# Cross attention in one core: the last key's term as one fp32r product for each half of the output

## What is computed

```python
xn = _layernorm(x, ln_gamma, ln_beta)
q = (xn @ w_q).reshape(B, SQ, NUM_HEADS, DIM_HEAD)
kv = context @ w_kv
k, v = jnp.split(kv, 2, axis=-1)
...
scores = jnp.einsum('bqhd,bkhd->bhqk', q * SCALE, k)
attn = jax.nn.softmax(scores, axis=-1)
out = jnp.einsum('bhqk,bkhd->bqhd', attn, v).reshape(B, SQ, INNER)
out = out @ w_out + b_out
```

## Time and profile before

| | us |
|---|---|
| median of three runs (lowest, highest) | 1835.36 (1833.28, 1838.26) |
| the profiled execution | 1835.1 |
| its span, first to last instruction | 1833.3 |
| TensorE busy | 1797.8 (98%) |
| VectorE busy | 1120.9 (61%) |
| ScalarE busy | 666.9 (36%) |
| GpSimd busy | 557.6 (30%) |

### The profile page before, as it was taken

One profiled execution on the slowest core, in us unless ns is written; L12 is line 12 of the kernel. 1 busy time (PEld: TensorE's weight loads), 2 busy tenths in 40 slices (PEclk: granted clock), 3 DMA queues, 4 the chain that ended last, 5 costly groups with the idle time before them and its releaser, 6 DMA issues.

```text
span 1833.3 us, 36324 instructions
## 1 busy us (share of the span) xinstructions
PE 1797.8 (98%) x13584; PEld 1547.6 (84%) x13584; DVE 1120.9 (61%) x2271; ACT 666.9 (36%) x1356; POOL 557.6 (30%) x546
## 2 busy tenths in 40 slices
PE   5999999999999999999999999999999999999999
PEld 4878988998899899889988997788887788888887
DVE  6636567666756765676667666788889733333322
ACT  2245444544454554445444544311112411111111
POOL 3024534544454355335434545411121000000000
PEclk9999999999999999999999999999999999999999
DMA  7325434543544354345434447432440502010100
GB/s 254 127 97 145 128 112 121 145 125 93 147 126 124 105 149 134 107 126 148 116 102 139 128 117 244 140 90 83 126 130 22 177 8 69 1 69 0 46 1 23
DMA packets 236118, 199.16 MB, mean 109 GB/s; under 512 B 12768, under 2 KB 193376, under 8 KB 236064
## 3 DMA queue, kind: packets, MB, share of 16 engines
q1 hardware_dynamic: 231632, 189.78, 35.8%
q10 hardware_dynamic: 4432, 8.65, 1.3%
HBM read 131.01 MB, written 33.82 MB: 90 GB/s over the span
## 4 chain that ended last, share of the span: by engine, by line
PE 90%; DVE 2%; DMA 1%; SPq 0%; issue 0%; POOL 0%; ACT 0%; DVEq 0%; POOLq 0%; ACTq 0%
PE s_ps L83 25%; PE s_ps L84 24%; PE s_ps L85 24%; PE s_ps L579 7%; PE s_ps L634 6%; PE s_ps L641 1%; PE s_ps L1365 1%; PE s_ps L1376 1%; PE s_ps L1307 0%; DMA a_m_xn<-x 0%; DMA a_xin<-x 0%; PE s_ps L588 0%; PE s_ps L1387 0%; PE s_ps L1356 0%; DMA o_lo<-x_o_lo 0%
## 5 line engine op out<-in xcount | busy, mean ns | idle before, releaser
L83 PE MATMUL s_ps<-w_cT_hi,w_space_hi 128*128 128x258 f32 x1024 | 293.3, 286 | 0.2 <-DVE w_space_lo L725 0.2
L84 PE MATMUL s_ps<-w_cT_lo,w_space_hi 128*128 128x258 f32 x1024 | 289.9, 283 | 0.0
L85 PE MATMUL s_ps<-w_cT_hi,w_space_lo 128*128 128x258 f32 x1024 | 288.3, 282 | 0.0
L530 POOL TENSOR_TENSOR x_prob<-x_prob,x_share 128x256 f32<-128x256 f32 x256 | 155.6, 613 | 338.4 <-DVE x_share L692 330.2
L718 DVE COPY x_mix<-s_ps 128x512 f32<-128x512 f32 x256 | 174.5, 687 | 68.6 <-PE s_ps L85 66.1
L83 PE MATMUL s_ps<-x_pT_hi,x_cn_hi 128*128 128x512 f32 x512 | 206.0, 402 | 4.0 <-DVE x_mix L718 4.0
L850 ACT ACTIVATE x_prob<-s_ps,x_negmax 128x257 f32<-128x257 f32 x256 | 121.9, 476 | 240.2 <-DVE x_negmax L687 237.0
L85 PE MATMUL s_ps<-x_pT_hi,x_cn_lo 128*128 128x512 f32 x512 | 201.4, 393 | 0.0
L84 PE MATMUL s_ps<-x_pT_lo,x_cn_hi 128*128 128x512 f32 x512 | 200.8, 392 | 0.0
L83 PEld LDWEIGHTS s_ps<-w_cT_hi,w_space_hi 128*128 128x128 f32 x1024 | 193.4, 189 | 6.2 <-issue 3.8
L84 PEld LDWEIGHTS s_ps<-w_cT_lo,w_space_hi 128*128 128x128 f32 x1024 | 193.9, 189 | 0.7
(11 more groups left out here) (204 smaller groups left out, 3526.7 us busy)
## 6 DMA issues: line engine op xcount, KB each, us to landing
e_raw_T<-ctx_T SPq DMA_DIRECT2D x64, 514.0 KB, 4.6
e_raw_n<-ctx_nat SPq DMA_DIRECT2D x64, 512.0 KB, 3.9
x_prob_T<-x_blocks SPq DMA_DIRECT2D x256, 128.0 KB, 2.7
q<-q_q ACTq DMA_DIRECT2D x16, 512.0 KB, 2.8
e_q<-q SPq DMA_DIRECT2D x16, 512.0 KB, 4.1
o_hi<-x_o_hi SPq DMA_DIRECT2D x32, 256.0 KB, 2.7
o_lo<-x_o_lo SPq DMA_DIRECT2D x32, 256.0 KB, 3.7
a_oT_hi<-o_hi SPq DMA_DIRECT2D x16, 512.0 KB, 4.2
```

What stands on the lines that cost most here:

```text
L83: pe.matmul(out, lhs[0], rhs[0], start=start, stop=False)
L84: pe.matmul(out, lhs[0], rhs[1], start=False, stop=False)
L85: return pe.matmul(out, lhs[1], rhs[0], start=False, stop=stop)
L530: pool.tensor_tensor(prob[:, i, 0:KT * P], prob[:, i, 0:KT * P], share[:, i:i + 1].to_broadcast([P, KT * P]), ALU.mult)\
```

## The change

The sixteen last-key products of a turn become two, one for each half. A product has 128 rows of contraction, of which 96 are used: `last_v` has, for each of four groups of heads and each of two (`l`), twelve rows: three for each of four batches. The three rows hold the high part of the values, the low part and the high part again, as `v_dram` now has them; the matching rows of `last_p` hold the probability's high part twice and its low part. The sum over rows is then high x high, high x low, low x high. Columns are the 512 of the bank, rows of the result the 128 of a head pair. The product opens the accumulation of the whole bank (`start=True`), and the value products add to it.

Around it: GpSimd writes each last probability three times. VectorE rounds the turned probabilities to fp32r (`last_h`), takes the rest, with sign and place from the new table `last_rows`, and spreads half by half: the first in `keep_last`, the second behind `low_out(t, 0)`. Ahead of the loop VectorE takes the low part of the values and three DMAs write them. `load_v` has eight DMAs and stands behind `load_n(t, 2)`. `out_half(0)` waits first for the loads, for the third copy of mix 3 and for `last_p`, and for the fourth copy where it needs that chunk.

```diff
-    last_p = s.sb("last_p", [P, TILES, GB, SQ])
-    last_v = s.sb("last_v", [P, inner])
-    last_z, last_t = s.sb("last_z", [P, TILES, SQ]), s.sb("last_t", [P, TILES, SQ])
-    own = s.sb("own", [P, GB])
+    last_p = s.sb("last_p", [P, 2, PAIRS // 2, GB, SQ], F32R)
+    last_v = s.sb("last_v", [P, 2, P], F32R)
+    last_z, last_t = s.sb("last_z", [P, TILES, SQ // 2]), s.sb("last_t", [P, 2, SQ])
+    last_h = s.sb("last_h", [P, 2, SQ], F32R)
+    OWN = GB * PAIRS // 2
+    own = s.sb("own", [P, OWN + 1])
...
             sp.wait_ge(o_ready.sem, o_ready.at(t, 0))
+            rows = v_rows[bass.ds(t * GB * PARTS, GB * PARTS), :].rearrange("r (m l g e) -> r m l g e", m=2, l=2, g=HT)
             for g in range(HT):
-                dst = last_v[g * SQ:g * SQ + GB, :].rearrange("b (i g e) -> b i g e", g=HT, e=HE)[:, :, g, :]
-                src = v_dram[bass.ds(t * GB, GB), :].rearrange("b (i g e) -> b i g e", g=HT, e=HE)[:, :, g, :]
-                sp.dma_start(dst, src).then_inc(v_loaded.sem, 16)
+                for l in range(2):
+                    at, h = g * SQ + l * SQ // 2, g % 2
+                    sp.dma_start(f32(last_v[at:at + GB * PARTS, :, h * HE:(h + 1) * HE]), rows[:, :, l, g, :])\
+                        .then_inc(v_loaded.sem, 16)

...
         def turn(t, more):
-            load_v(t)
             if more:
...
             load_n(t, 2)
+            load_v(t)
             if more:
...
-        for g in range(HT):
-            sp.dma_start(own[g * SQ:(g + 1) * SQ, :], identity[0:SQ, 0:GB]).then_inc(own_loaded, 16)
+        sp.dma_start(own[:, :], last_rows).then_inc(own_loaded, 16)
...
-        sp.wait_ge(v_stored, 16)
+        sp.wait_ge(v_stored, 48)
...
-            pool.tensor_tensor(last_z[:, :, b % GB], prob[:, :, SK - 1], share[:, :], ALU.mult)\
+            at = b % GB * PARTS
+            pool.tensor_tensor(last_z[:, :, at:at + PARTS], prob[:, :, SK - 1:SK].to_broadcast([P, TILES, PARTS]),
+                               share[:, :].rearrange("p (i k) -> p i k", k=1).to_broadcast([P, TILES, PARTS]), ALU.mult)\
...
         def out_half(t, m):
+            if m == 0:
+                pe.wait_ge(v_loaded.sem, v_loaded.at(t, 16 * 2 * HT))
+                pe.wait_ge(mix_kept.sem, mix_kept.at(t, GB * DC - 1))
+            pe.wait_ge(last_kept.sem, last_kept.at(t, m + 1))
+            pe.matmul(ps[:, O_BANK[m], :], last_v[:, m, :], last_p[:, m, :, :, :].rearrange("p j b q -> p (j b q)"),
+                      start=True, stop=False)
             for j in range(4 * m, 4 * m + 4):
...
                 for c in range(DC):
-                    if j == 0:
-                        pe.wait_ge(mix_kept.sem, mix_kept.at(t, (GB - 1) * DC + max(c + 1, DC - 1)))
+                    if j == 0 and c == DC - 1:
+                        pe.wait_ge(mix_kept.sem, mix_kept.at(t, GB * DC))
                     for h in range(2):
                         n = 2 * j + h
-                        pe.matmul(out[h], w_v[:, c, n * HE:(n + 1) * HE], mix[:, c, :, place(n)],
-                                  start=c == 0, stop=False)
-                if j == 0:
-                    pe.wait_ge(v_loaded.sem, v_loaded.at(t, 16 * HT))
-                    pe.wait_ge(last_kept.sem, last_kept.at(t, 1))
-                for h in range(2):
-                    n = 2 * j + h
-                    mm = pe.matmul(out[h], last_v[:, n * HE:(n + 1) * HE],
-                                   last_p[:, n // HT, :, :].rearrange("p b q -> p (b q)"), start=False, stop=True)
+                        mm = pe.matmul(out[h], w_v[:, c, n * HE:(n + 1) * HE], mix[:, c, :, place(n)],
+                                       start=False, stop=j == 4 * m + 3 and c == DC - 1)
             mm.then_inc(o_ready.sem, 1)
...
             dve.wait_ge(last_ready.sem, last_ready.at(t, GB))
-            dve.transpose(last_t[:, :, :], last_z[:, :, :]).then_inc(last_turned.sem, 1)
+            dve.transpose(last_t[:, :, :], last_z[:, :, :].rearrange("p (m l) r -> p m (l r)", m=2))\
+                .then_inc(last_turned.sem, 1)
             dve.wait_ge(last_turned.sem, last_turned.at(t, 1))
+            dve.tensor_copy(last_h[:, :, :], last_t[:, :, :]).then_inc(last_turned.sem, 1)
+            dve.wait_ge(last_turned.sem, last_turned.at(t, 2))
+            dve.scalar_tensor_tensor(last_t[:, :, :], last_t[:, :, :], own[:, OWN:OWN + 1], f32(last_h[:, :, :]), ALU.mult,
+                                     ALU.add).then_inc(last_turned.sem, 1)
+            dve.wait_ge(last_turned.sem, last_turned.at(t, 3))
             dve.wait_ge(o_ready.sem, o_ready.at(t, 0))
-            dve.tensor_tensor(last_p[:, :, :, :],
-                              last_t[:, :, :].rearrange("p i (b q) -> p i b q", b=1).to_broadcast([P, TILES, GB, SQ]),
-                              own[:, :].rearrange("p (i b q) -> p i b q", i=1, q=1).to_broadcast([P, TILES, GB, SQ]),
+            spread_last(t, 0)
+
+        def spread_last(t, m):
+            shape = [P, OWN, SQ]
+            dve.tensor_tensor(last_p[:, m, :, :, :].rearrange("p j b q -> p (j b) q"),
+                              last_t[:, m, :].rearrange("p (x q) -> p x q", x=1).to_broadcast(shape),
+                              own[:, 0:OWN].rearrange("p (x q) -> p x q", q=1).to_broadcast(shape),
                               ALU.mult).then_inc(last_kept.sem, 1)
...
             low_out(t, 0)
+            spread_last(t, 1)
             if more:
...
-        dve.wait_ge(own_loaded, 16 * HT)
+        dve.wait_ge(own_loaded, 16)
+        dve.wait_ge(v_rounded, 1)
+        dve.tensor_tensor(all_last[1], ps[0:B, M_BANK[0]:M_BANK[0] + 2, :], f32(all_last[0]), ALU.subtract)\
+            .then_inc(v_copied, 1)
...
-        act.activation(all_last, ps[0:B, M_BANK[0]:M_BANK[0] + 2, :], ACT.Copy).then_inc(v_copied, 1)
+        act.activation(all_last[0], ps[0:B, M_BANK[0]:M_BANK[0] + 2, :], ACT.Copy).then_inc(v_rounded, 1)
+        act.wait_ge(v_rounded, 1)
+        for k in (0, 2):
+            act.dma_start(v_dram[:, k, :].rearrange("b (h n) -> b h n", h=2), f32(all_last[0])).then_inc(v_stored, 16)
...
-        act.dma_start(v_dram.rearrange("b (h n) -> b h n", h=2), all_last).then_inc(v_stored, 16)
+        act.dma_start(v_dram[:, 1, :].rearrange("b (h n) -> b h n", h=2), f32(all_last[1])).then_inc(v_stored, 16)
...
+    last_rows = np.zeros((4, 2, 16, 17), np.float32)
+    for g, l, b, k in itertools.product(range(4), range(2), range(4), range(3)):
+        last_rows[g, l, 3 * b + k, 4 * (2 * l + g // 2) + b] = -1 if k == 2 else 1
+        last_rows[g, l, 3 * b + k, 16] = -1 if k == 2 else 0
```

More of the change, by code:

```diff
@@ L374, in cross_attention @@
     share_done, probs_ready = s.count("share_done", GB * TILES), s.count("probs_ready", GB * TILES)
-    last_ready, last_turned = s.count("last_ready", GB), s.count("last_turned", 1)
+    last_ready, last_turned = s.count("last_ready", GB), s.count("last_turned", 3)
     turned = s.count("turned", GB * TILES)
@@ L378, in cross_attention @@
     pT_hi, pT_lo = s.count("pT_hi", GB * KT), s.count("pT_lo", GB * KT)
-    last_kept = s.count("last_kept", 1)
+    last_kept = s.count("last_kept", 2)
     mixed, mix_kept = s.count("mixed", GB * DC), s.count("mix_kept", GB * DC)
@@ L383, in cross_attention @@
     o_stored = s.count("o_stored", 64, 32)
-    l_loaded, v_ready, v_copied, v_stored = s.sem("l_loaded"), s.sem("v_ready"), s.sem("v_copied"), s.sem("v_stored")
-    all_last, lT = mix[0:B, 0, 0:2, :], mix[:, 1, 0, 0:DC * B].rearrange("p (c b) -> p c b", c=DC)
+    l_loaded, v_ready, v_rounded = s.sem("l_loaded"), s.sem("v_ready"), s.sem("v_rounded")
+    v_copied, v_stored = s.sem("v_copied"), s.sem("v_stored")
+    all_last, lT = [mix[0:B, 0, 2 * k:2 * k + 2, :].bitcast(F32R) for k in range(2)], mix[:, 1, 0, 0:DC * B].rearrange("p (c b) -> p c b", c=DC)
     slots = [wk[:, j, :] for j in range(PAIRS)]
@@ L556, in gpsimd @@
         pool.memset(last_z[:, :, :], 0.0)
-        for ap in [last_v[:, :]] + [f32(a[:, :, SK:SKE]) for c in cT for a in c]:
+        for ap in [f32(last_v[:, :, :])] + [f32(a[:, :, SK:SKE]) for c in cT for a in c]:
             last = pool.memset(ap, 0.0)
@@ L752, in turn @@
             invert(t, 1, 3)
[L753 removed]
+            dve.wait_ge(v_stored, 48)
             keep_mix(t, 0, 0)
@@ L1757, in build @@
 def build(nc, x, ctx_nat, ctx_T, last_T, gamma, beta, wq, wkT, wv, w_out, b_out, gate, aq, ak, av, wg, wu, wd,
-          identity, same_token, out):
+          identity, same_token, last_rows, out):
     tokens, dim = x.shape
@@ L1813 @@
 def kernel(**inputs):
+    import itertools
     import numpy as np
```

13 lines of the change are left out of this document (7 added, 6 removed).

## The result

The changed kernel took **1852.9 us** (median of 4 runs, 1850.3 to 1856.3) against 1834.4 us (1833.3 to 1838.3) of the kernel before on the same chip: 1.0094 times as long, 95% interval 1.0082 to 1.0106. The forecast was 1819 us, faster. It came out on the other side. The profiled execution took 1854.4 us, its span is 1852.3 us, 19.0 more than before.

A forecast was written before the change was run, and what follows sets the result against it. TensorE, busy in all of a 62.9 us turn, was taken as the bound. 15 turns x (1.50 gained - 0.30 waited) = 18.0, less 1.4 in the last turn, is 16.6 us off: 1819 us, range 1811 to 1831.

The forecast's parts named there:

- The removed and the added products: TensorE's output halves: four last-key pairs out, one 0.23 us product in; with a covered stall, 1.50 us gained a turn.
- Rival 4: Opening product of each output half costs 0.43 us instead of 0.23; 31 lose 6 us: 1825 us, chance 0.07.
- The stall in the first block: First output half, VectorE's last copy of `mix` late by 0.21 to 0.25 us; new product ahead gains 0.20 a turn.
- What VectorE gets: `keep_last` gains two steps, 0.5 us together, and a second spread comes behind `low_out(0)`; both covered by VectorE's idle time.
- The moved and doubled loads: Eight value loads hold SP 6.6 us, exchange of batch 2 goes 1.5 us late; TensorE waits 0.3 us a turn.
- rival 3: Eight issues hold SP longer than the products save, deciding from 7.8 us; up to 1857 us, slower; chance 0.06.
- Rival 2: Context of batch 2 lands late, so TensorE waits 1.0 or 1.5 us: 1829 us (chance 0.10) or 1836 (0.08).
- rival 1: Eight loads on SP are covered, issuing in under about 6.2 us, so no TensorE wait: 1814 us, chance 0.19.
- The last turn: No fold pairs hide the loads: exchange 2.7 us late, 2.0 count, 0.9 given back, 0.3 charged between halves; 1.4 lost.
- Ahead of the loop and in the first turn: VectorE's subtraction of 64x1024 values, about 1.3 us, runs beside the first score tiles: 0 counted (bounds 0 and 1.3).

## Why the prediction was wrong

**The removed and the added products: right, a little too good.** 1.50 us a turn were counted, and the kernels without a wait give 62.87 - 61.57 = 1.30. From the last mix product to the first value product 0.33 us passed before (626.77 to 627.10) and 0.71 pass now (697.21 to 697.92), so the opening product costs 0.38 us in the first half where 0.23 was taken. In the second half the same count gives 0.24 (709.28 to 709.73, against 639.53 to 639.74), as forecast: the 0.33 us behind the product there are what a 512-column fp32r product ahead of fp32 products took in the kernel before too. Rival 4 named this mechanism at 0.43 for both halves and priced it at 6 us; it came in one half of two, 0.15 us a turn of the 0.20 that are missing. The stall in the first block of the earlier trace rows did go: the 64 products take 3.65 and 3.64 us in the two halves (697.92 to 701.57, 709.73 to 713.37).

**What VectorE gets: right in the loop, wrong in the last turn.** `keep_last` and the spread are in VectorE's timeline:

```profile
691.14 0.20 DVE L740 CAST x_last_h<-x_last_t 128x64 fp32r<-128x64 f32 x1
691.37 0.28 DVE L742 SCALAR_TENSOR_TENSOR x_last_t<-x_last_t,x_own,x_last_h 128x64 f32<-128x64 f32 x1
691.78 0.69 DVE L750 TENSOR_TENSOR x_last_p<-x_last_t,x_own 128x512 fp32r<-128x512 f32 x1
...
694.89 0.69 DVE L725 COPY x_mix<-s_ps 128x512 f32<-128x512 f32 x1 [0.61 <-PE s_ps L85]
...
1135.16 1.06 DVE L740 CAST x_last_h<-x_last_t 128x64 fp32r<-128x64 f32 x1
1136.26 1.26 DVE L742 SCALAR_TENSOR_TENSOR x_last_t<-x_last_t,x_own,x_last_h 128x64 f32<-128x64 f32 x1
1137.55 1.66 DVE L750 TENSOR_TENSOR x_last_p<-x_last_t,x_own 128x512 fp32r<-128x512 f32 x1
```

In the loop the two added steps take 0.64 us (691.14 to 691.78) where 0.5 were forecast, and VectorE still idles 0.61 us behind them, as it had 0.69. In the last turn the same three steps take 1.06, 1.26 and 1.66 us instead of 0.20, 0.28 and 0.69. The prediction priced them nowhere in that turn, though the kernel before has a hint: its one spread took 1.48 us there, at 1123.38. They stand ahead of the copy that ends the wait of 2.38 us, and that wait is theirs and not the loads'. From TensorE's restart behind the wait before it to its end 5.39 us pass (1134.47 to 1139.86), and 5.37 to 5.40 in each of the other ten runs that have the three steps, with loads in that turn or without. In the kernel before with the eight loads, which lacks the two added steps, it is 2.90 us and there is no wait. Where the granted clock is low in that stretch the products fill more of the 5.4 us, and the wait shrinks to between 0.8 and 1.2 us, in one run to nothing.

**The moved and doubled loads: the step that failed, and in it one term.** The chain was laid out right: SP, exchange, ScalarE's probabilities, VectorE's `split_probs(2)` and copies, TensorE at the third chunk of the mix of batch 2. Its slack was right too: 1.5 us late gives 0.3 us, and the split loads in the kernel before measured 1.5 and 0.33. Wrong was the price of one issue. "The nearest rows for their pace are the four themselves", 0.83 us apart; but those had 4 partitions and the new ones have 12, and these came 0.99 apart. Eight of them hold the queue 7.92 us instead of 6.6, the 1.3 us have no cover left, and the wait is 1.35 us and 0.1 for the restart on top. The prediction's own threshold was close: it set the point of decision at 7.8 us, 0.98 each. At the measured 7.92 its rule gives a wait of 1.6 us and a turn 0.1 us longer; it is 0.29 longer, since the products gave 1.30 and not 1.50. The case had been rival 3, at 0.06. The row against it, the median of 0.64, was of loads of another shape; the 0.63 to 1.12 of its spread should have been the bound, with the chance to match.

That context and exchange together decide is seen in ScalarE's 2.50 and 0.56 us: the context's landing ended the longer idle time, and the exchange landed 0.56 us behind its rounding. Rival 2 took its delay from a slow landing; it came from the late issue.

The Trainium skill ("DMA: Bandwidth & Descriptors", Anatomy of one DMA) puts the sequencer's dispatch at about 50 ns, in a table on DMAs that GpSimd issues. The prediction took it over to loads that SyncE issues. The runs have 0.562 to 0.785 us for these, so it was no support for rival 1.

**The last turn: 1.4 us lost was forecast, some 9 measured.** The lateness of the exchange was right, 2.7 us forecast and 2.8 measured (1107.37 to 1116.65, against 1098.35 to 1104.83), but it was priced once, at 2.0 us. What came: three waits on `x_mix` of 2.99, 2.03 and 2.38 us for the one of 3.96, the third of them VectorE's; between the halves 3.11 us where 0.3 was charged (bounds 0 and 4), because nothing stands there to hide the spread that waits for `low_out(0)`; and a lower clock for part of the last mix (products 0.43 us apart from 1140.58 to 1143.56) and, 2.5 us, in the second half. The wait between the halves was named, at 2 us, and then priced near its lower bound. The early spread measured it: 5.9 us with its clock. Of the 9.2 us about half comes without any load: the last turn lasts 63.0 us before, 72.2 after, and 67.6 in the run that loads the values once (1076.50 to 1144.07).

**Ahead of the loop and in the first turn.** 0 was taken for VectorE's subtraction, with a bound of 1.3, and 0 is right. The first turn starts 1.25 us later than before, but that lateness is there at the first fold already, ahead of the subtraction: 120.21 us before, 121.48 after, and 27.0 us from there to the first mix in both. The run with the loads in the idle queue has the same program up to its first mix, and starts it at 146.29 us. So this is scatter between executions. The first turn was counted as any other; it has waits of 2.13 and 0.46 us, a granted clock of 0.53 from 177.5 to 181.0 us, and lost 3.0 us.

Sum of the misses: 15 turns that lose 0.29 us instead of gaining 1.20 are 22 us, the first turn 3 more, the last turn 8, the scatter ahead of the loop 1 and what is behind the cross attention 1: the 35 us between 1819 and the profiled execution's 1854.4.

## What to carry to other kernels

The time for which a queue's sequencer is held by issues is a resource like an engine's: count the issues in front of each transfer that someone waits for, and take their price from loads of the same shape or bound it by the longest of the line, above all where the step decides the sign. The same loads cost 3.3, 1.6 or 0 us a turn in three places of one queue; look for the stretch in which the queue idles before making them smaller or fewer. A last turn has lost its fillers: whatever the loop hides must be priced there again, with the clock that follows a wait.

## What was not expected of the hardware

- The issue of a small DMA did not follow its bytes: 0.62 us for 2 partitions of 4 pieces, 0.64 for 4 of 4, **0.78 for 12 of 2**, 0.56 for 16 of 2 and 0.60 for 32 of 2, pieces of 256 bytes each. Which property of 12 makes it dear was not found; three, six or eight partitions were not tried.
- Some of VectorE's instructions took up to five times as long in the last turn (0.20 to 1.06, 0.28 to 1.26, 0.69 to 1.66 us). Two things are new there, the weights coming in and GpSimd working on them, and the trace of the changed kernel tells them apart. It has the same operation in the same shape twice, then the busy times around each (columns as in the earlier trace rows):

```profile
1139.73 1.15 DVE L398 TENSOR_TENSOR w_cT_lo<-e_wk,w_cT_hi 128x512 fp32r<-128x512 f32 x1
...
1143.13 0.68 DVE L398 TENSOR_TENSOR w_space_lo<-e_wk,w_space_hi 128x512 fp32r<-128x512 f32 x1
...
1139.00:1142.00 3.00, 2.14 (x6) 1.72 (x7) 3.00 (x5) 0.21 (x1) 3.00 (x2) 0.71 0.07 7
1142.00:1145.00 3.00, 3.00 (x15) 2.16 (x15) 2.31 (x4) 0.00 (x0) 0.02 (x1) 0.72 0.87 239
```

It is slow with GpSimd busy throughout (3.00 of 3 us) and DMA at 7 GB/s, and fast with GpSimd idle (0.02) and DMA at 239 GB/s. So the slowness goes with GpSimd's work and not with the traffic. Copies out of PSUM kept their 0.68 us beside it (1139.13 us). No run took GpSimd's work away.

- The fp32r product that opens the first output half, behind mix products, took 0.42 us to the fp32 products behind it; in the second half, behind score products, it took the 0.33 us that such a product takes ahead of fp32 ones elsewhere. Back to back it is 0.23. Moving two of the three semaphore waits ahead of the first one left the 0.42 as it was.
- A wait of TensorE of 2.3 us in the loop was followed in some turns by 3 us at a granted clock of about 0.5 and in others by none: with the eight loads at the head the turns took 64.1 and 65.5 us by turns. The waits of 1.14 to 1.50 us of the changed kernel were followed by no such stretch in any of the turns behind the first.
